# Constants of VectorE's compares in a PSUM bank of their own, in a kernel of two graph layers

## The reference

```
h  = relu(layernorm(x))                       # layer 0, a GCN
w' = dinv[src] * w * dinv[dst]                # self loops added, dinv = 1/sqrt(degree)
x  = x + relu(segment_sum(w' * (h @ K)[dst], src) + bias)
h  = relu(layernorm(x))                       # layer 1
m_fwd  = concat(h[src], edge_attr) @ W_fwd + b_fwd    # summed at dst
m_back = concat(h[dst], edge_attr) @ W_back + b_back  # summed at src
agg = segment_sum(both) / count
x  = x + gamma * norm(leaky(agg) + h) + beta
```

## Time and profile before

| | us |
|---|---|
| median of 3 runs | 4618.35 (4617.26 to 4620.77) |
| profiled execution, its time | 4623.39 |
| profiled execution, its span | 4621.6 |
| TensorE busy | 3497.9 (76%) |
| VectorE busy | 3319.0 (72%) |
| ScalarE busy | 1864.9 (40%) |
| GpSimd busy | 2905.8 (63%) |

### The profile page before, as it was taken

The page is one execution under the profiler, slowest core; times in us unless marked ns, Lnnn a source line. Parts: engine busy times, 40 slices in busy tenths (PEclk is TensorE's granted clock), DMA queues, the critical chain, the costliest instruction groups (busy, mean ns, idle before and its releaser), DMA issues. The chain is left out here.

```text
span 4621.6 us, 103887 instructions
## 1 busy us (share of the span) xinstructions
PE 3497.9 (76%) x32143; PEld 2940.4 (64%) x32143; DVE 3319.0 (72%) x8239; ACT 1864.9 (40%) x4498; POOL 2905.8 (63%) x1711
## 2 busy tenths in 40 slices
PE   3555307988988888889991359989889889899955
PEld 2545306777777777777770347767767767777645
DVE  8999728878888888888881477766666666666427
ACT  1011005545555555555550424444444444444513
POOL 0000076888888888888883068877888777788300
PEclk8777658999999999999995659999999999999977
DMA  9990116777777777777778655555555545555761
GB/s 167 304 132 0 43 22 134 137 134 145 139 134 139 137 135 138 136 135 136 138 139 129 122 103 83 81 81 77 81 81 79 80 75 79 78 82 82 90 126 28
DMA packets 678459, 503.84 MB, mean 109 GB/s; under 512 B 305948, under 2 KB 591012, under 8 KB 676296
## 3 DMA queue, kind: packets, MB, share of 16 engines
q0 software_dynamic: 256832, 174.75, 34.5%
q1 hardware_dynamic: 421092, 322.34, 29.1%
HBM read 283.21 MB, written 240.09 MB: 113 GB/s over the span
## 5 line engine op out<-in xcount | busy, mean ns | idle before, releaser
L707 POOL DMA_INDIRECT gcn_sums<-fl_sums,fl_to_i x864 | 1470.1, 1702 | 307.4 <-DMA gcn_sums<-fl_sums,fl_to_i 151.7
L1535 POOL DMA_INDIRECT gcn_sums<-shared,ds_to_i x752 | 1303.3, 1733 | 533.4 <-ACT shared L1787 319.9
L1742 PE MATMUL bank<-ds_counts,ds_parts 128*128 128x256 bf16 x3675 | 605.9, 278 | 0.0
L1811 ACT COPY ds_turned<-bank 128x1024 bf16<-128x1024 bf16 (+1 forms) x325 | 313.1, 963 | 602.1 <-PE bank L1727 503.7
L931 ACT COPY fl_sums<-bank 128x256 f32<-128x256 f32 x864 | 324.0, 375 | 558.0 <-PE bank L859 416.0
L1775 ACT CAST ds_counts<-bank 128x392 bf16<-128x392 f32 x800 | 382.7, 490 | 225.7 <-PE bank L1686 204.5
L744 DVE SCALAR_TENSOR_TENSOR fl_same<-fl_key_b,fl_pat,from_me 128x128 f32<-128x128 bf16 x864 | 374.1, 445 | 132.0 <-PE bank L859 110.2
L1762 PE MATMUL bank<-ds_turned,ds_now 128*128 128x512 bf16 (+1 forms) x1950 | 463.4, 375 | 0.0
L372 PE MATMUL bank<-places,row_hot 128*128 128x200 bf16 x1616 | 268.4, 293 | 254.3 <-DVE places L325 254.3
L1671 DVE TENSOR_TENSOR src_sums<-src_sums,bank 128x512 f32<-128x512 f32 (+1 forms) x325 | 213.3, 656 | 259.3 <-PE bank L1762 254.5
L1704 PE MATMUL bank<-shared 128*128 128x128 f32 x1504 | 307.7, 309 | 116.7 <-DVE attr_sums L1588 88.1
(11 more groups left out here) (236 smaller groups left out, 7786.0 us busy)
## 6 DMA issues: line engine op xcount, KB each, us to landing
fl_attrs<-in_edge_attr SPq DMA_DIRECT2D x108, 512.0 KB
shared<-in_edge_attr SPq DMA_DIRECT2D x186, 256.0 KB
fl_rel_b<-dst_offset SPq DMA_DIRECT2D x108, 256.0 KB
fl_key_b<-src_key SPq DMA_DIRECT2D x108, 256.0 KB
gcn_sums<-zeros SPq DMA_DIRECT2D x40, 640.0 KB
shared<-src_key SPq DMA_DIRECT2D x94, 256.0 KB
gcn_sums<-fl_sums,fl_to_i POOLq DMA_INDIRECT x864
near<-src_float SPq DMA_DIRECT2D x1, 12892.0 KB
```

The source lines that it names most:

```text
L707: nc.gpsimd.indirect_dma_start(out=d.tab_gcn[j % K], out_offset=bass.IndirectOffsetOnAxis(ap=to_i[:, (GPI * kk + gi) % 4, j:j + 1], axis=0 ...
L1535: nc.gpsimd.indirect_dma_start(out=d.tab_gcn[j % K].rearrange("n (two f) -> (n two) f", two=2), out_offset=bass.IndirectOffsetOnAxis(ap=to ...
L1742: ins = nc.tensor.matmul(row_bank[:, 0:2 * P], parts[:, tile, s, :], counts[:, h, tile, :, :].rearrange("p b q -> p (b q)"), start=(tile = ...
```

## The change

A PSUM bank, `const_bank`, holds constants that VectorE's compares read: in `first_layer` the numbers 0 to 127 (`iota_c`), the mask (`from_me_c`) and ones (`ones_c`), in `dense_sums` the first two. They are copied there once at the start of each. `spread_hot` is made with scalar_tensor_tensor (compare, then times ones) in place of tensor_scalar. The bank comes from the pairs in `first_layer`, which have one bank then, and from the way back in `dense_sums`, which has one. The waits follow: a batch of pairs waits for the copy of the batch before it, a way-back product for the add of the block before it.

```diff
...
-        pair_bank, turn_bank, prod_bank = d.bank[4:6], d.bank[6], d.bank[7]
+        pair_bank, const_bank, turn_bank, prod_bank = d.bank[4], d.bank[5], d.bank[6], d.bank[7]
+        iota_c, from_me_c, ones_c = (const_bank[:, k * P:(k + 1) * P] for k in range(3))
...
-        numbers_ready, twos_ready, hot_ready, hi_ready = sem("numbers_ready"), sem("twos_ready"), sem("hot_ready"), sem("hi_ready")
+        const_ready, twos_ready, hot_ready, hi_ready = sem("const_ready"), sem("twos_ready"), sem("hot_ready"), sem("hi_ready")
...
-                nc.vector.tensor_tensor(sum_hot[:], d.iota[:].unsqueeze(1).to_broadcast([P, J, P]), rec[:, h, 2, :].unsqueeze(2).to_broadcast([P, J, P]),
+                nc.vector.tensor_tensor(sum_hot[:], iota_c.unsqueeze(1).to_broadcast([P, J, P]), rec[:, h, 2, :].unsqueeze(2).to_broadcast([P, J, P]),
...
-                nc.vector.scalar_tensor_tensor(same[:, j, :], key_p[:, h, :, j], pat_f[:, j:j + 1], d.from_me[:],
+                nc.vector.scalar_tensor_tensor(same[:, j, :], key_p[:, h, :, j], pat_f[:, j:j + 1], from_me_c,
-                    nc.vector.tensor_scalar(spread_hot[:], rel_b[:, h, :, :].rearrange("p q j -> p j q"), d.part[:, 0:1], None,
-                                            ALU.is_equal).then_inc(spread_ready, 1)
+                    nc.vector.scalar_tensor_tensor(spread_hot[:], rel_b[:, h, :, :].rearrange("p q j -> p j q"), d.part[:, 0:1],
+                                                   ones_c.unsqueeze(1).to_broadcast([P, J, P]), ALU.is_equal, ALU.mult).then_inc(spread_ready, 1)
...
-            nc.vector.tensor_copy(numbers[:], d.iota[:]).then_inc(numbers_ready, 1)
-            dve.wait_ge(numbers_ready, 1)
+            nc.vector.tensor_copy(iota_c, d.iota[:]).then_inc(const_ready, 1)
+            nc.vector.tensor_copy(from_me_c, d.from_me[:]).then_inc(const_ready, 1)
+            nc.vector.tensor_copy(ones_c, d.ones[:]).then_inc(const_ready, 1)
+            nc.vector.tensor_copy(numbers[:], d.iota[:]).then_inc(const_ready, 1)
+            dve.wait_ge(const_ready, 4)
...
-                at_least(pe, pair_copied, BATCHES * k + n - 1)
+                at_least(pe, pair_copied, BATCHES * k + n)
-                        last = nc.tensor.matmul(pair_bank[at][:, c * HH:(c + 1) * HH], lo_hot[:, go % 2, q, :], hi_w[:, go % 2, m, q, :], start=(m == 0), stop=(m == 2))
+                        last = nc.tensor.matmul(pair_bank[:, c * HH:(c + 1) * HH], lo_hot[:, go % 2, q, :], hi_w[:, go % 2, m, q, :], start=(m == 0), stop=(m == 2))
...
-                nc.scalar.copy(to, pair_bank[n % 2][:, 0:PB * HH].rearrange("p (c k) -> p k c", c=PB)).then_inc(pair_copied, 1)
+                nc.scalar.copy(to, pair_bank[:, 0:PB * HH].rearrange("p (c k) -> p k c", c=PB)).then_inc(pair_copied, 1)
...
-        pair_bank, row_bank, back_bank = d.bank[0:2], d.bank[2], d.bank[3:5]
+        pair_bank, row_bank, back_bank, const_bank = d.bank[0:2], d.bank[2], d.bank[3], d.bank[4]
+        iota_c, from_me_c = const_bank[:, 0:P], const_bank[:, P:2 * P]
...
-                nc.vector.tensor_tensor(sum_hot, d.iota[:].unsqueeze(1).to_broadcast([P, J, P]), rec[:, p, 2, :].unsqueeze(2).to_broadcast([P, J, P]),
+                nc.vector.tensor_tensor(sum_hot, iota_c.unsqueeze(1).to_broadcast([P, J, P]), rec[:, p, 2, :].unsqueeze(2).to_broadcast([P, J, P]),
...
-                nc.vector.scalar_tensor_tensor(same[:, j, :], key_p[:, p, :, j], pat_f[:, j:j + 1], d.from_me[:],
+                nc.vector.scalar_tensor_tensor(same[:, j, :], key_p[:, p, :, j], pat_f[:, j:j + 1], from_me_c,
...
+            link(nc.vector.tensor_copy(iota_c, d.iota[:]))
+            link(nc.vector.tensor_copy(from_me_c, d.from_me[:]))
...
-                    nc.vector.tensor_tensor(here, here, back_bank[(BLOCKS * h + b) % 2][:, 0:n], ALU.add).then_inc(src_added, 1)
+                    nc.vector.tensor_tensor(here, here, back_bank[:, 0:n], ALU.add).then_inc(src_added, 1)
...
-                    if not (first and b < 2):
-                        pe.wait_ge(src_added, u - 1)
+                    if not (first and b == 0):
+                        pe.wait_ge(src_added, u)
-                            ins = nc.tensor.matmul(back_bank[v][:, 0:n], now[:, h, half, s, :], turned[:, v, half, 0:n],
+                            ins = nc.tensor.matmul(back_bank[:, 0:n], now[:, h, half, s, :], turned[:, v, half, 0:n],
...
```

## The result

The changed kernel takes 4672.34 us in the median of 4 runs (4666.37 to 4677.76), the kernel before 4617.81: a ratio of 1.0122, interval [1.0106, 1.0139], so +54.5 us where I forecast +24. A second comparison with more runs of before gave 4673.92 against 4621.02, 1.0113 [1.0094, 1.0132]. Slower, as forecast, and inside the range of 4590 to 4690, but above the 4628 to 4665 that I gave the forecast itself, and by twice the size.

What follows compares the result with a forecast made beforehand. The first layer's pass was taken as bound by the TensorE-VectorE chain in its middle and GpSimd at its end, the second layer by TensorE. +40 - 34 + 16 + 2 = +24 us gave 4642, own range 4628 to 4665, full range 4590 to 4690.

Steps and rivals of the forecast that it cites:

- the spread's duration: First layer, L749: 2.03 us against 1.23, +0.80 us in each of 108 groups, 87 us of VectorE's time.
- its price in the kernel as it was: First layer: VectorE's later one-hots expose 1.54 us of TensorE's time per slot, 26 slots: +40 us, bounds 0 and +106.
- the starts: Start of the layers: five copies of constants and the first spread's 0.80 us, for which TensorE stands: +2 us.
- the pairs' bank: First layer: TensorE waits for the copy just before, with 2.9 us of room: zero, up to +5 us.
- the mask: L744 and L1601, mask from PSUM: -6 ns each, 5 us of VectorE per layer; the keys' stride price of 93 ns stays.
- the scatters' new mean: First layer, GpSimd: mean scatter falls from 1702 ns to near 1.63 us, about half of 119 us of stretching gone.
- TensorE's wait for the one-hots: First layer: TensorE's wait on VectorE's L783, 87.8 us before, would be near 128 us.
- The way-back bank: Second layer, block 6: L1762 waits for VectorE's add (L1671), 18 tiles x 0.90 = +16 us, bounds +5 and +25.
- the term of -34 us for what GpSimd gains: First layer: scatters gain 60 us, counted only in TensorE's staging waits and the tail; bounds 0 and -42.
- The tail, -19: End of first layer: 27.2 us behind the last staged chunk shrink to about 8, the scatters' queue then being short.
- The wait for staging, -15: First layer's middle: GpSimd's gain counts where TensorE waits for staging copies, 14.8 us.
- Rival 2: First layer: scatters bound more than seen, nearly all GpSimd gains counts, -60 us; 4591, faster; chance 0.12.

Runs made afterwards that it cites:

- the relief alone: Kernel before with first-layer numbers and mask in PSUM and one bank of pairs, old spread and old second layer: 4597.50 us, 0.9971.
- The halved scatters: First-layer scatters over 64 partitions in place of 128: on the kernel before 4570.63 us, 0.9914; on the changed kernel 4652.45 us, 1.0086.
- the measured forms: Changed kernel with ten forms of VectorE's compares, 16 times each, added before the first layer's loop; one execution, 4842 us.
- the spread edge by edge: Kernel before with the spread's compare written in line and TensorE's weights read with a step of 8 columns: 4674.75 us, 1.0115.

## Why the prediction was wrong in size

What it had right: the spread's duration (2.03 us worked out, 2.085 measured) and its price in the kernel as it was (+42 with the starts, measured +34 alone); the pairs' bank (0, measured +3 with an interval that holds 0); the mask (-6 ns, measured -3 to -4) and with it that the stride's price stays; the scatters' new mean (1.63 us, measured 1.62). TensorE's wait for the one-hots was to be near 128 and is 116. For the scatters' mean I gave L749 a share as one that reads SBUF twice; it reads one tensor, but scatters that start in it are stretched all the same (last section). The way-back bank has the right number (+16, measured +17), but not by the working shown: 11 to 13 products wait, not 18, and for too little (below).

**The step that failed is the term of -34 us for what GpSimd gains.** It was mis-sized: on top of the new spread it measures -7 (+27 against +34), not clear of nothing, and without the new spread -13. With -7 in its place the sum is +40 - 7 + 16 + 2 = +51, against a measured +52 to +54. That the sum comes so near is partly luck, since the measured parts are +34, -7 and +17, together +44.

The term had two halves, and they failed in two ways.

*The tail, -19.* This part is not there even without the new spread: with the relief alone the tail is 27.2 us, as before. In the last slot, which has no pairs, the chunks of these kernels come every 1.44 to 1.45 us in the mean (2.0 to 2.2 in most slots), faster than a scatter and its gap of 0.3, so the queue fills again though it was nearly empty before. In the kernel with the relief alone 0.5 to 1.7 chunks wait in slots 16 to 25 and 13 at the last copy. With the new spread alone, scatters at 1710 ns, the tail is 20.5; with the relief on top it is 18.8, 21.9 and 21.1 in three traces. The end of the changed kernel's pass in the timeline:

```profile
2475.02 0.37 ACT L935 COPY fl_sums<-bank 128x256 f32<-128x256 f32 x1 [0.30 <-PE bank L863]
...
2490.71 1.56 POOL L708 DMA_INDIRECT gcn_sums<-fl_sums,fl_to_i  x1 [0.30 <-issue]
2492.57 1.58 POOL L708 DMA_INDIRECT gcn_sums<-fl_sums,fl_to_i  x1 [0.30 <-issue]
```

The last scatters are at their shortest, 1.86 us from start to start, and still end 18.8 us behind the copy: nine chunks wait there.

*The wait for staging, -15.* This I read from the kernel before and credited to the shorter scatters, beside a spread that takes it away by itself: with the new spread alone no wait for the staging copies is left among TensorE's. What the relief adds there has no more wait to remove. The row is a weak sign besides: with one bank of pairs alone it falls from 14.8 to 1.0 us, and the time stays.

So the pass isn't a sum of a TensorE-VectorE term and a GpSimd term. Both pull on one path, the later one counts, and the overlap must be taken off once. The halved scatters show it: they give the kernel before 40 us and the changed one 12 to 17, a part of it perhaps by the clock. I had already priced the spread in the state of before, where part of its delay falls into time in which the scatters hold TensorE; the relief would have had to be priced in the state after. Taken the other way round, relief first, the spread would have had to be priced at its +58 and not at +26 to +35.

Rival 2 had half of this: the scatters do hold more than the 14.8 us that TensorE's waits name, 40 to 51 us. It failed by its condition, since it took the relief in full beside a spread that had already emptied the queue.

By stage the two traces of the changed kernel show +34 and +38 to the last copy, -8 and -5 in the tail behind it, -6 and -1 between the last scatter and the second layer's start, and +23 and +21 in the second layer. The last is more than the +16 of the forecast, and why I leave open. From its first to its last instruction the second layer takes 1790.0 to 1792.0 us in three traces with its whole change, 1787.3 with the way-back bank alone, and 1760.2 to 1772.2 in five traces where it is as before, so it is mostly the bank's cost and not the constants'. But TensorE's waits on the add name only 3 to 5 us, where I foresaw some 16. Matmul records that are missing may hide some. Two layers measured apart give 27 + 17 = 44 of the 52; each has an interval of some 7 us either way, so the missing 8 is not shown to be anything.

VectorE's stride price has the size that the Trainium skill gives ("Vector Engine (DVE) Microarchitecture Reference", section "5.2 Measured stream behaviour on trn2": 1.73 ns an element for a source that hops, measured there on 4-byte words and far hops): L823 and L829 differ by 0.72 ns an element on top of some 1.05, 1.77 together. The one-tensor compare pays less, 1131 ns for all of its 1024 elements (L825). The other page that I weighed ("VectorE: DVE Perf Modes", section "The TRN2 errata — SBUF-src ops pay a fixed extra latency per instruction") would have each operand's move to the bank cost an estimated 65 ns; the measured forms say 4 ns less in the small form and 12 less in 2031.

## What to carry to other kernels

Where two engines can each be the late one, don't add a gain on the one to a loss on the other: take the loss first, ask how much of the other's queue is left, and credit only that. A queue's depth at the copies that feed it, and its empty time, tell which state one is in; the waits by name do not, since they had 15 us where 40 to 51 were held. Before crediting anything to a queue's tail, look at the pace at which it is fed at the very end: here that pace, and not the state before it, fills it. And price a form of an instruction by stride and by number of operands before giving up a one-operand compare: in line the second tensor cost 0.53 us here, with the stride 0.89.

## What the runs showed that I had not expected

- A scatter over 64 partitions takes 1.41 to 1.42 us, one over 128 takes 1.56 (medians): between the two, half of the rows save a tenth of an indirect DMA's price on GpSimd.
- A load of f32 weights with a step of 8 numbers takes 335 ns in place of 192, and the product with it 402 in place of 275. So a stride is cheaper on VectorE's side here: 378 ns a group there by the forms, against 127 ns on each of sixteen products.
- Which scatters are stretched goes by what VectorE reads when they start. Here the first layer's scatters are grouped, out of four traces, by VectorE's instruction that was running at their start (number of scatters, their mean in ns; lines of the kernel before; `SBUF` and `bank` say where the numbers or the mask were):

| running at the start | before | spread alone | numbers and mask alone | changed |
|---|---|---|---|---|
| numbers' compare (L720) | 51, 2159 SBUF | 90, 2220 SBUF | 45, 1562 bank | 53, 1561 bank |
| key compare (L744) | 199, 1668 SBUF | 251, 1603 SBUF | 225, 1583 bank | 181, 1561 bank |
| spread (L749) | 23, 2338 old form | 107, 1562 new form | 77, 2148 old form | 107, 1561 new form |
| weighing (L783) | 141, 1748 | 56, 1765 | 130, 1709 | 116, 1673 |

So the numbers' compare stretches a scatter by 0.6 us from SBUF and not from the bank, and the new spread stretches none. The old spread does, though it reads only one tensor, so "two tensors from SBUF" is not the whole condition. With the new spread alone the mean over all scatters stays at 1710 ns, because 90 scatters and not 51 start in the numbers' compare. The mean depends on such timing too: with the spread edge by edge, and numbers and mask in SBUF, it is 1629.
